# A token tower on one core: preparing steps with the transposed rows taken ahead, the second normalisation on ScalarE, and the small constant summed as a 65th element

## What is computed

```
h = W.T[x] + b + pe                                        # embedding and positions
h = h + attn(layernorm(h))                                 # 8 heads of 16, linear, causal, with running mean and variance
h = h + ffn(layernorm(h), E = 8 experts of 512)            # layernorm again, then
    hx = layernorm(layernorm(h)) * ln_g + ln_b
    q, k, v = hx @ Wq, hx @ Wk, hx @ Wv                    # 2 heads of 64
    q = q / sqrt(sum(q*q) + 1e-12) * 8 * qn_g              # k likewise with kn_g
    o = softmax(causal(q k^T / 8)) v ;  y = o @ Wo
    out = sum_e softmax(y @ gate_W + gate_b)_e * (gelu(y @ W1_e + b1_e) @ W2_e + b2_e)
```

## Time and profile before

| | |
|---|---|
| median of three runs | 852.5 us |
| the profiled execution's own time | 850.87 us |
| span of its trace | 849.1 us |
| busy: TensorE, VectorE, ScalarE, GpSimd | 92%, 84%, 56%, 40% of the span |
| granted TensorE clock, mean | 0.978 of full speed |
| preparing steps | from 226 to 285 us of the span |

### The profile page before, as it was taken

One profiled execution on the slowest core, in us unless ns is written; L12 is line 12 of the kernel. 1 busy time (PEld: TensorE's weight loads), 2 busy tenths in 40 slices (PEclk: granted clock), 3 DMA queues, 4 the chain that ended last, 5 costly groups with the idle time before them and its releaser, 6 DMA issues.

```text
span 849.1 us, 21002 instructions
## 1 busy us (share of the span) xinstructions
PE 777.6 (92%) x8208; PEld 555.6 (65%) x8208; DVE 710.1 (84%) x1585; ACT 478.3 (56%) x997; POOL 341.3 (40%) x386
## 2 busy tenths in 40 slices
PE   2799999999876789998889889999999999999997
PEld 1668887788644455555556556777777777777775
DVE  3668899888489776776777878999999999999997
ACT  2436555555255667776879666455555555555553
POOL 6649999777365557666667530000000000000000
PEclk9899999999799999999999999999999999999999
DMA  3101011000000000000000000000000000000000
GB/s 130 56 8 35 23 38 38 25 26 17 10 1 1 1 2 2 2 3 2 2 14 3 2 2 2 2 14 2 14 1 14 2 14 2 14 2 14 2 14 14
DMA packets 9666, 12.09 MB, mean 14 GB/s; under 512 B 1856, under 2 KB 6592, under 8 KB 9568
## 3 DMA queue, kind: packets, MB, share of 16 engines
q1 hardware_dynamic: 8544, 8.65, 3.4%
q0 software_dynamic: 1024, 2.10, 0.9%
HBM read 8.65 MB, written 2.10 MB: 13 GB/s over the span
## 4 chain that ended last, share of the span: by engine, by line
PE 75%; DVE 9%; ACT 7%; issue 5%; POOL 2%; DMA 1%; DVEq 0%; ACTq 0%; POOLq 0%
PE ps L988 73%; DVE mx L834 2%; DVE room L944 1%; ACT room L562 1%; DVE room L942 1%; ACT room L553 1%; ACT qk L492 1%; DMA h_all<-emb_rows,idx 1%; DVE mx L829 1%; PE ps L1016 1%; DVE och L911 0%; ACT qh L499 0%; PE ps L996 0%; ACT kh L501 0%; ACT hxT L481 0%
## 5 line engine op out<-in xcount | busy, mean ns | idle before, releaser
L577 ACT ACTIVATE cst<-ps,col 128x512 f32<-128x512 f32 x256 | 176.1, 689 | 164.0 <-PE ps L988 163.2
L988 PEld LDWEIGHTS ps<-arena,sq 128*128 128x128 f16 x3072 | 192.2, 98 | 62.1 <-DVE sq L972 4.2
L988 PE MATMUL ps<-arena,sq 128*128 128x128 f16 x3072 | 213.1, 219 | 0.5 <-DVE sq L972 0.5
L988 PE MATMUL ps<-y,arena 128*128 128x512 f16 x768 | 208.7, 382 | 1.3 <-DVE och L911 1.3
L972 DVE TENSOR_TENSOR sq<-cst,sq 128x512 f16<-128x512 f32 x256 | 175.8, 687 | 4.4
L373 POOL TENSOR_TENSOR room<-room 128x512 f16<-128x512 f32 (+3 forms) x122 | 123.6, 1032 | 74.2 <-ACT room L562 72.6
L967 DVE CAST sq<-cst 128x512 f16<-128x512 f32 x256 | 108.9, 425 | 11.5 <-ACT cst L577 4.2
L553 ACT ACTIVATE room<-ps 128x512 f32<-128x512 f32 (+3 forms) x160 | 76.7, 533 | 41.3 <-PE ps L988 40.9
L834 DVE TENSOR_REDUCE mx<-ps 128x2 f32<-128x1024 f32 (+2 forms) x64 | 70.1, 1096 | 30.4 <-PE ps L988 30.2
L988 PEld LDWEIGHTS ps<-y,arena 128*128 128x128 f16 x768 | 65.0, 98 | 34.0 <-issue 3.4
L960 DVE SCALAR_TENSOR_TENSOR h_all<-ps,gs,h_all 128x128 f32<-128x128 f32 x256 | 77.2, 344 | 1.0 <-PE ps L988 0.9
(11 more groups left out here) (158 smaller groups left out, 1186.9 us busy)
## 6 DMA issues: line engine op xcount, KB each, us to landing
sq<-w_rows SPq DMA_DIRECT2D x16, 256.0 KB, 2.8
out<-h_all SPq DMA_DIRECT2D x32, 64.0 KB, 1.6
cst<-consts SPq DMA_DIRECT2D x1, 896.0 KB, 5.3
h_all<-emb_rows,idx POOLq DMA_INDIRECT x32, 2.6
cst<-consts SPq DMA_DIRECT2D x1, 398.0 KB, 3.3
c<-consts SPq DMA_DIRECT2D x1, 256.0 KB, 5.1
wqkv<-w_qkv SPq DMA_DIRECT2D x1, 192.0 KB, 3.4
wsm<-w_sm SPq DMA_DIRECT2D x1, 192.0 KB, 5.1
```

Source lines behind the costliest of these rows:

```text
L577: a.activation(hid[:, f], ps[:, HBANK[f], :], ACT.Gelu_apprx_tanh, bias=col[:, K_B1 + k:K_B1 + k + 1], scale=1.0 / WS).then_inc(S["hid_rea ...
L988: return t_.matmul(o, l, r, start=start, stop=stop, skip_group_check=True)
```

## The change

Six edits. (1) `normed_T(c+3)` moves ahead of `project2(c+2)` on TensorE and ahead of `squares(c+2)` on ScalarE, for c from 1; two waits for shared PSUM banks are moved by a chunk with it. (2) `normed2` for chunks 3 to 15 goes from VectorE to ScalarE, where it stands last in the step and one chunk further ahead (`normed2(c+4)`); `normed2(3)` stands before the first step. Chunks 0 to 2 stay on VectorE. (3) For it VectorE writes the negated mean (one small instruction more in `stats2`) and GpSimd multiplies it by the factor (one small instruction and one wait more in `both_norms`). (4) `qk2` gets a 65th column that holds 1e-12, written once by GpSimd; the sum runs over 65. (5) `l2_factors` loses its addition. (6) One small memset at the start goes and one comes later.

```diff
--- before.py
+++ after.py
@@ -63,8 +63,7 @@
         b2s = sb("b2s", [4 * E, 4 * D])
         mhalf = sb("mhalf", [P, 16])
         qkg8 = sb("qkg8", [P, 1])
-        eps = sb("eps", [P, 10])
-        ln_eps, l2_eps = eps[:, 0:2], eps[:, 2:10]
+        ln_eps = sb("eps", [P, 2])[:]
         credit = sb("credit", [P, 16])
         h_all = sb("h_all", [P, T, D])
         kh = sb("kh", [P, B * N], F16)
@@ -129,13 +128,13 @@
 
         st2 = sb("st2", [P, 2, B, 6])
         mv2 = sb("mv2", [P, NT, B, 2])
-        rr = sb("rr", [P, NT, 2, B])
+        rr = sb("rr", [P, NT, 4, B])
         x2_all = sb("x2", [P, 2, B, D])
         hxT_all = sb("hxT", [P, 2, B, P])
         x2 = [x2_all[:, i] for i in range(2)]
         hxT = [hxT_all[:, i] for i in range(2)]
-        qk2 = sb("qk2", [P, B, 4 * DS])
-        ss = sb("ss", [P, 2, 3, B * 4])
+        qk2 = sb("qk2", [P, B * 4, DS + 1])
+        ss = sb("ss", [P, 2, 2, B * 4])
         qkn = sb("qkn", [P, B, 4 * DS])
 
         mx = sb("mx", [P, 2, 4, NQ, HS])
@@ -160,7 +159,7 @@
         gT = sb("gT", [4 * E, P])
         sqf = sq[:].rearrange("p b h j -> p (b h j)")
         stage = [sqf[:, 0:512], sqf[:, 512:1024]]
-        scaled = [qkn[:].rearrange("p b e -> p (b e)"), qk2[:].rearrange("p b e -> p (b e)")]
+        scaled = [qkn[:].rearrange("p b e -> p (b e)"), qk2[:].rearrange("p g e -> p (g e)")[:, 0:512]]
         hid = cst[:, C_POS:C_POS + 4 * CH].rearrange("p (u t) -> p u t", u=4)
         hhi = sqf[:, 0:2 * CH].bitcast(F16).rearrange("p (u t) -> p u t", u=4)
         hlo = sqf[:, 2 * CH:4 * CH].bitcast(F16).rearrange("p (u t) -> p u t", u=4)
@@ -176,7 +175,7 @@
             vhi_ready vlo_ready qkd_ps hi_ready lo_ready sm_ps sm_used max_link mneg mrow_ps mrow_sb s_ps
             s_used p_ready phi_dve plo_pool plo_dve pv_done o_link o_used oT_ps oT_sb y_ps yhi_ready ylo_ready
             lg_ps lg_link lg_ready eg_ready gate_ready gT_ps gT_sb b2_ps h2_ready hid_ps hid_ready hhi_ready
-            hlo_even hlo_odd l2_link x_sb v_link ao_link w2_done eo_used stored"""
+            hlo_even hlo_odd neg2 eps_set x_sb v_link ao_link w2_done eo_used stored"""
         S = {name: sem(name) for name in names.split()}
         GATHERED = [sem(f"gathered{c}") for c in range(NT)]
         NPIECE = 2 * E * FF // 512
@@ -238,9 +237,8 @@
             gather(0, B)
             g.memset(mhalf[:], -0.5).then_inc(S["setup"], 1)
             g.memset(ln_eps, LN_EPS).then_inc(S["setup"], 1)
-            g.memset(l2_eps, L2_EPS).then_inc(S["setup"], 1)
             gather(B, 2 * B)
-            pool.wait_ge(S["setup"], 3)
+            pool.wait_ge(S["setup"], 2)
 
             def front(c, par):
                 pool.wait_ge(S["stats"], c + 1)
@@ -291,7 +289,9 @@
 
             def both_norms(c):
                 pool.wait_ge(S["stats2"], c + 1)
-                g.tensor_tensor(rr[:, c, 1], rr[:, c, 0], mhalf[:, 0:B], ALU.pow).then_inc(S["rr_ready"], 1)
+                g.tensor_tensor(rr[:, c, 1], rr[:, c, 0], mhalf[:, 0:B], ALU.pow).then_inc(S["neg2"], 1)
+                pool.wait_ge(S["neg2"], c + 1)
+                g.tensor_tensor(rr[:, c, 3], rr[:, c, 1], rr[:, c, 2], ALU.mult).then_inc(S["rr_ready"], 1)
 
             front(0, 0)
             gather(4, 6)
@@ -302,7 +302,7 @@
             front(1, 1)
             g.memset(v16[:, :, :, DS:DS + 1], 1.0).then_inc(S["setup"], 1)
             g.memset(mpad[:], 0.0).then_inc(S["setup"], 1)
-            pool.wait_ge(S["setup"], 10)
+            pool.wait_ge(S["setup"], 9)
             pool.wait_ge(S["load_a"], 32)
             out_bias(0)
             out_bias(1)
@@ -334,15 +334,14 @@
             def l2_factors(c):
                 par = c % 2
                 pool.wait_ge(S["ss_ready"], c + 1)
-                g.tensor_tensor(ss[:, par, 1], ss[:, par, 0], l2_eps, ALU.add).then_inc(S["l2_link"], 1)
-                pool.wait_ge(S["l2_link"], c + 1)
-                g.tensor_tensor(ss[:, par, 2], ss[:, par, 1], mhalf[:, 0:8], ALU.pow).then_inc(S["rn_ready"], 1)
+                g.tensor_tensor(ss[:, par, 1], ss[:, par, 0], mhalf[:, 0:8], ALU.pow).then_inc(S["rn_ready"], 1)
 
             both_norms(NT - 5)
             coefs(NT - 3)
             state_add(NT - 2)
             for n in WAT[NT - 3]:
                 weights_low(n)
+            g.memset(qk2[:, :, DS:], L2_EPS).then_inc(S["eps_set"], 1)
             out_bias(NT - 1)
             both_norms(NT - 4)
             coefs(NT - 2)
@@ -489,7 +488,9 @@
                     act.wait_ge(S["ss_ready"], c)
                 else:
                     act.wait_ge(S["wlow_ready"], NEARLY - 1)
-                a.activation(qk2[:], ps[:, q:q + B, 0:2 * D], ACT.Square).then_inc(S["sqqk"], 1)
+                a.activation(qk2[:, :, 0:DS].rearrange("p (b g) e -> p b g e", b=B),
+                             ps[:, q:q + B, 0:2 * D].rearrange("p b (g e) -> p b g e", e=DS), ACT.Square
+                             ).then_inc(S["sqqk"], 1)
                 a.copy(v16[:, 2 * c:2 * c + B, :, 0:DS],
                        ps[:, q:q + B, 2 * D:3 * D].rearrange("p b (h d) -> p b h d", h=HS)).then_inc(S["vhi_ready"], 1)
 
@@ -510,14 +511,28 @@
             squares(1)
             normed_T(2)
 
+            def normed2(c):
+                act.wait_ge(S["rr_ready"], c + 1)
+                act.wait_ge(S["x2T_ps"], c - 1)
+                for b in range(B):
+                    last = a.activation(x2[c % 2][:, b], h_all[:, 2 * c + b, :], ACT.Identity,
+                                        bias=rr[:, c, 3, b:b + 1], scale=rr[:, c, 1, b:b + 1])
+                last.then_inc(S["x2_ready"], 1)
+
             def step_b(c):
+                if c and c + 3 < NT:
+                    normed_T(c + 3)
                 if c + 2 < NT:
                     squares(c + 2)
                 high_qk(c)
                 if c == 4:
                     ao_out(NT - 1)
-                if c + 3 < NT:
-                    normed_T(c + 3)
+                if c == 0:
+                    normed_T(3)
+                if c + 4 < NT:
+                    normed2(c + 4)
+
+            normed2(3)
 
             for c in range(BTAIL):
                 step_b(c)
@@ -733,8 +748,8 @@
                     last = v.bn_aggr(mv2[:, c, b], st2[:, par, b])
                 last.then_inc(S["agg2"], 1)
                 dve.wait_ge(S["agg2"], c + 1)
-                v.tensor_scalar(rr[:, c, 0], mv2[:, c, :, 1], 1.0 + LN_EPS, LN_EPS * LN_EPS, ALU.mult, ALU.add
-                                ).then_inc(S["stats2"], 1)
+                v.tensor_scalar(rr[:, c, 0], mv2[:, c, :, 1], 1.0 + LN_EPS, LN_EPS * LN_EPS, ALU.mult, ALU.add)
+                v.tensor_scalar(rr[:, c, 2], mv2[:, c, :, 0], -1.0, None, ALU.mult).then_inc(S["stats2"], 1)
 
             def step_a(c, nxt, more=2, first=False):
                 cur = 1 - nxt
@@ -770,7 +785,9 @@
 
             def sum_squares(c):
                 dve.wait_ge(S["sqqk"], c + 1)
-                v.tensor_reduce(ss[:, c % 2, 0], qk2[:].rearrange("p b (g e) -> p (b g) e", e=DS), AX, ALU.add
+                if c == 0:
+                    dve.wait_ge(S["eps_set"], 1)
+                v.tensor_reduce(ss[:, c % 2, 0], qk2[:], AX, ALU.add
                                 ).then_inc(S["ss_ready"], 1)
 
             def low_v(c):
@@ -787,7 +804,7 @@
                     dve.wait_ge(S["qkd_ps"], c)
                 v.tensor_tensor(qkn[:].rearrange("p b (g e) -> p b g e", e=DS),
                                 ps[:, q:q + B, 0:4 * DS].rearrange("p b (g e) -> p b g e", e=DS),
-                                ss[:, c % 2, 2].rearrange("p (b g) -> p b g", b=B).unsqueeze(3)
+                                ss[:, c % 2, 1].rearrange("p (b g) -> p b g", b=B).unsqueeze(3)
                                 .to_broadcast([P, B, 4, DS]), ALU.mult).then_inc(S["qkn_ready"], 1)
 
             def low_qk(c):
@@ -850,8 +867,6 @@
                     sum_squares(c + 1)
                 if c == 0:
                     h1_out(NT - 2)
-                if c + 3 < NT:
-                    normed2(c + 3)
                 if 0 <= c - 6 < 8:
                     single_max(c - 6)
                 if c:
@@ -1057,7 +1072,7 @@
             project(1, 1)
             for b in range(B):
                 project_rows(1, 1, b)
-            pe.wait_ge(S["setup"], 10)
+            pe.wait_ge(S["setup"], 9)
             pe.wait_ge(S["dt_sb"], B)
             sums(0, 0, 0, first=True)
             for b in range(B):
@@ -1122,9 +1137,9 @@
                     pe.wait_ge(S["h1_ready"], NT - 1)
                 if c > 3:
                     pe.wait_ge(S["hxT_sb"], c)
-                if c == 7:
+                if c == 8:
                     pe.wait_ge(S["aoT_sb"], NT)
-                if c == 8:
+                if c == 9:
                     pe.wait_ge(S["h1_ready"], NT)
                 for b in range(B):
                     last = t_.transpose(ps[:, x2_bank(c), b * P:(b + 1) * P], x2[c % 2][:, b], ident)
@@ -1180,18 +1195,20 @@
```

(10 more changed lines are left out.)

## The result

The changed kernel took 862.43, 862.57, 862.68 and 865.31 us, a median of 862.62 against 852.18 of four runs of the kernel before; the ratio is 1.0134 with an interval of 1.010 to 1.0168. A second measurement, further down, gave 1.0107 (1.0075 to 1.014). The forecast was 857.4 with a range up to 862.0. The direction was right, the size was too small (4.9 us forecast, 10.4 between the medians), and the range ended just short of the result.

The account below looks back on a forecast made before the run. ScalarE's loop of waits was taken to bound the preparing steps, 3.72 us growing to 4.30 with the pair in it. The differences over the steps summed to +4.9 us, 857.4 against the median of 852.5; range 851.5 to 862.

Parts of the forecast that it names:

- The new wait: Preparing steps: ScalarE's two normalising instructions, then two transposes, hold up the next projection in place of hxT; 0.513 us each instruction.
- Its size: Regular preparing steps: new tail of 1.13 us against 0.55, so +0.58 a step, a period of 4.30 for 3.72.
- 2 to 3: Between projections of chunks 2 and 3: pair, hand-over and transposes come behind hxT's end, +1.03 us.
- 6 to 8: Between projections of chunks 6 and 8: two periods plus ao copy and output projection, 9.01 for 8.52 us, +0.49.
- The last step: Projections of chunks 14 to 15: no pair left in ScalarE's step, the 3.02 us loop binds, -0.70.
- GpSimd's multiplication: Ahead of `coefs` in each first attention step, behind `l2_factors` in the others: about 0.3 us with its wait, costing nothing.
- first attention and experts unchanged: Sign that the forecast is right: outside the preparing steps, first attention and experts keep their times.
- Rival B: Preparing steps: clock falls as TensorE idles; seven projections 1.1 to 1.5 us longer, 865, or 860 for two or three; chance 0.15.
- The profiled execution: Profiled run of the kernel before, 850.87 us, 1.6 below the median of 852.5; its like was forecast at 855.8.
- The 65th element: Constant in the sum for GpSimd's addition: 0.3 us off GpSimd's loop, some 2.75 a chunk, hidden under 4.30.
- Rival C: Preparing steps: pair does not bind, steps fall to the 3.02 us loop over `unit_qk` and `unit_T`; -7.4, 845; chance 0.07.
- A: Preparing steps: pair is cheap, adds 0.37 us, period 3.89; about +0.2, 852.7; chance 0.18 including cases up to half a per cent.

Follow-up runs that it names:

- the mended kernel: Changed kernel with ScalarE's pair ahead of the squares: 851.10 us; with GpSimd's multiplication also done once after the first attention: 848.98 us. Regular steps 3.04 in both.
- a third profile: Changed kernel with GpSimd's multiplication for chunks 3 to 12 taken out of the first attention and done once ahead of the preparing steps: 860.45 us, ratio 1.0102.

## Why the prediction was right and wrong

- **The new wait**: right. The pair at the end of ScalarE's step, the transposes behind it, hxT out of the loop: chain and waits show it as written. The pair's instruction was 503 ns for 513.
- **Its size**: 4.19 for the predicted 4.30. The hand-over to the transposes was 0.05 for 0.10, and the squares start 1.51 after the projection for 1.56. With 2 to 3 at 4.91 in place of 5.25 and 6 to 8 at 8.78 in place of 9.01, the stretch without the clock grew 3.4 us where the terms named had 4.8; the pair's term was too large by that. The last step came at 2.95 for 3.02.
- **GpSimd's multiplication**: this is the step that failed, and with it the line "first attention and experts unchanged". I put it at nothing because "behind it wait only instructions that wait for VectorE longer". That holds in the late steps of the first attention, where GpSimd waits 2.67 us for VectorE, and not while gathers are issued. There its list was full to 11.92 us, and the 0.4 was paid in seven steps: 2.5 us from the fourth normalisation to the last, and 2.8 to 3.4 where the clock fell once besides. The gaps of TensorE that I had named as a sign of this came (9.78 us busy of 10). In the earlier trace rows GpSimd's 133.9 of 167 us looks like room; it is a mean over steps with and without gathers.
- **The clock**: this is the second step that failed: the sum held nothing for it. Rival B came, with a chance of 0.15 and a size about right for three steps (I had 860 for two or three). It was there in both profiles of the changed kernel, worth 3.0 us each time, so it deserved to stand in the forecast: the 1.8 us of idling that I had worked out stood next to the 2.07 after which the clock had fallen. What decides in which steps it falls is open: with the same idle times it fell in three steps, in three and in one.
- **The profiled execution**: that of the kernel before had an early start, 2.6 us ahead of its next profile at the third normalisation. Sums made against it are not touched by that, but the comparison of starts was.
- **The 65th element**: hidden, as said; 0.3 us each in the two steps that GpSimd bounds, as said. What covers it I had wrong: without ScalarE's loop it is worth 0.28 a step.
- **Rival C's number**, 3.02, was nearly what the mended kernel gives (3.04), from another loop: `unit_qk`, sum of squares, power. The loop over GpSimd, which I had closing every second chunk at 2.9 each, closes every chunk, because the next chunk's sum stands behind `unit_qk` in VectorE's list. I had also said that taking the pair off VectorE would gain nothing in a loop near 3 us; with the pair back there the steps are 3.16 to 3.29 and the chain goes through it.
- **Two sums of the rivals**: in A, twice GpSimd's 4.1 against 8.67 is -0.5 and not -0.7, which makes A +0.4. In B, seven times 1.1 to 1.5 is 7.7 to 10.5, so that 865 is its low end. Neither changes a chance or the range.
- **A page's rule against the change**: the Trainium skill's "ScalarE: Activation LUTs", section "Rules for kernel authors", would have the pair on VectorE. On VectorE it is the shorter (0.51 on the chain against 0.77), yet in the right place ScalarE's costs nothing and VectorE's 0.1 to 0.25 a step. So the profiles speak against the rule here, by the place in the list and not by the price; the totals of the two kernels are the same.

In sum: GpSimd 2.5, clock 3.0, pair 3.4 to 4.1 (stretches without a fallen clock of 57.6 and 57.8 us against 53.7 to 54.2), 8.9 to 9.6 us together, against measured ratios that mean 9.1 and 11.4. The forecast had 4.9: the pair somewhat too large, the other two, 5.5 us, not at all.

## What to carry to other kernels

Work made a step earlier helps only if its producer's place in every queue is a step earlier too; look for the last instruction of one engine's step that the first of another's waits for, and try it ahead of the wait that the engine has anyway. Before calling an engine's time free, look at it in each kind of step, not in one and not in the mean: an engine whose list has no wait for others is full, however short of 100% its busy time is. And when a loop is taken away, write down the next one with the order of each queue in it, since an instruction that stands behind another belongs to its loop.

## What the runs showed of the hardware that was not expected

- The clock can fall in short idling too: with TensorE idle 1.4 to 1.75 us in each 4.19 us step it came to 0.67 over 10 us (a mix of its levels of 1.2 and 2.4 GHz), at the same three steps in both profiles of the changed kernel, but in one step only in a third profile with the same idle times. With four filling products a step and 0.6 to 0.9 us idle it stayed at 1.00, in two kernels.
- Two VectorE normalisations of 128x128 take 0.60 us in one piece early on and 1.86 us in the first attention's steps, while GpSimd works on large tiles. GpSimd's small multiplication takes 0.45 us in three of the steps there and 0.20 to 0.26 in the others and in the preparing steps. What makes both slower there wasn't tried.
- The third chunk's start differs by up to 8 us among all thirteen profiles, by 2.6 us between two of the same kernel, where the granted clock from 40 to 43 us was 0.90 and 0.50. A single profile is no measure of the start.
